# Four scan tiles at the start of an adaLN, attention and FFN kernel: the division by an estimate and one Newton step, and clippings moved to GpSimd

## The reference

```
tf    = sigmoid(sum(time_emb, -1))
decay = exp(-exp(w)) * (0.5 + 0.5*tf)
ek    = exp(min(k, 30));  ekv = ek * v
nf, df = forward scans  a = a*decay + ekv,  b = b*decay + ek
nb, db = the same scans in reverse
euk   = exp(min(u + k, 30))
num   = nf + nb - ekv + euk*v
den   = df + db - ek + euk
out   = sigmoid(r) * num / max(den, 1e-8) * (0.8 + 0.2*tf)
x1    = x + attention(out)          # 16 heads, segments of 128, memory with the delta rule
y     = x1 + ffn(scan2(x1, f, f))   # silu(z W1) * (z W3), Hadamard transform, W2
```

## Time and profile before

| | |
|---|---|
| median of 3 runs | 1583.58 us (1582.86 to 1585.2) |
| profiled execution, span | 1581.4 us |
| PE busy | 1547.0 us, 98% |
| DVE busy | 1219.7 us, 77% |
| ACT busy | 782.1 us, 49% |
| POOL busy | 615.2 us, 39% |

### The profile page before, as it was taken

The page is one execution under the profiler, slowest core; times in us unless marked ns, Lnnn a source line. Parts: engine busy times, 40 slices in busy tenths (PEclk is TensorE's granted clock), DMA queues, the critical chain, the costliest instruction groups (busy, mean ns, idle before and its releaser), DMA issues.

```text
span 1581.4 us, 26868 instructions
## 1 busy us (share of the span) xinstructions
PE 1547.0 (98%) x9574; PEld 1377.9 (87%) x9574; DVE 1219.7 (77%) x2719; ACT 782.1 (49%) x1687; POOL 615.2 (39%) x433
## 2 busy tenths in 40 slices
PE   4899999999999999999999999999999999999999
PEld 2699989999999999998999999989888888888887
DVE  8889888787878888778775773665897888687785
ACT  3576566445535626535546552653554443344442
POOL 3666585322222222222001000134664465666662
PEclk9999999999999999999999999999999999999999
DMA  5375685595473485474467547348211222311111
GB/s 177 124 246 191 223 292 195 180 392 184 161 276 127 154 286 201 147 254 160 174 228 280 210 171 283 110 141 279 88 54 54 60 89 72 107 46 62 54 41 54
DMA packets 109381, 262.04 MB, mean 166 GB/s; under 512 B 11200, under 2 KB 36160, under 8 KB 107840
## 3 DMA queue, kind: packets, MB, share of 16 engines
q1 hardware_dynamic: 90384, 227.28, 40.5%
q10 hardware_dynamic: 18864, 33.04, 6.5%
HBM read 212.03 MB, written 48.25 MB: 165 GB/s over the span
## 4 chain that ended last, share of the span: by engine, by line
PE 90%; DVE 6%; issue 2%; DMA 1%; ACT 1%; POOL 0%; SPq 0%; ACTq 0%; DVEq 0%
PE psG L595 17%; PE psG L597 17%; PE psG L596 17%; PE psX L771 4%; PE psX L726 3%; PE psX L595 3%; PE psX L597 3%; PE psX L596 3%; PE psZ L752 3%; PE psZ L743 3%; PE psZ L751 2%; PE psZ L597 2%; PE psY L597 2%; PE psY L596 2%; PE psZ L596 2%
## 5 line engine op out<-in xcount | busy, mean ns | idle before, releaser
L2076 POOL TENSOR_TENSOR wl<-stage,wh 128x512 fp32r<-128x512 f32 x160 | 233.5, 1481 | 147.4 <-ACT wh L1597 144.7
L595 PE MATMUL psG<-yh,wh 128*128 128x512 f32 x646 | 263.1, 407 | 0.0
L597 PE MATMUL psG<-yh,wl 128*128 128x512 f32 x646 | 253.0, 392 | 0.0
L596 PE MATMUL psG<-yl,wh 128*128 128x512 f32 x646 | 252.1, 390 | 0.0
L2144 POOL TENSOR_TENSOR vs<-v,omb 128x512 f32<-128x512 f32 x64 | 92.1, 1460 | 388.9 <-PE psX L726 216.0
L597 PEld LDWEIGHTS psG<-yh,wl 128*128 128x128 f32 x646 | 121.3, 188 | 26.8
L595 PE MATMUL psG<-wh,yh 128*128 128x256 f32 x480 | 141.6, 295 | 0.0
L595 PEld LDWEIGHTS psG<-yh,wh 128*128 128x128 f32 x646 | 121.9, 189 | 20.9 <-DVE sg L1274 0.3
L596 PEld LDWEIGHTS psG<-yl,wh 128*128 128x128 f32 x646 | 121.9, 189 | 20.5
L597 PE MATMUL psG<-wh,yl 128*128 128x256 f32 x480 | 135.7, 283 | 0.0
L596 PE MATMUL psG<-wl,yh 128*128 128x256 f32 x480 | 135.7, 283 | 0.0
(11 more groups left out here) (279 smaller groups left out, 4291.6 us busy)
## 6 DMA issues: line engine op xcount, KB each, us to landing
wh<-high_o SPq DMA_DIRECT2D x52, 512.0 KB, 3.6
wl<-low_o SPq DMA_DIRECT2D x52, 512.0 KB, 4.7
stage<-in_w SPq DMA_DIRECT2D x64, 256.0 KB, 3.1
wh<-high_k SPq DMA_DIRECT2D x23, 512.0 KB, 3.7
wl<-low_k SPq DMA_DIRECT2D x23, 512.0 KB, 5.0
wh<-high_q SPq DMA_DIRECT2D x23, 512.0 KB, 4.1
wl<-low_q SPq DMA_DIRECT2D x23, 512.0 KB, 5.8
wh<-high_v SPq DMA_DIRECT2D x22, 512.0 KB, 4.0
```

What stands on the lines that cost most here:

```text
L595: e.matmul(out, lh, rh, start=first, stop=False, skip_group_check=check)
L596: e.matmul(out, lh, rl, start=False, stop=False, skip_group_check=check)
L597: return e.matmul(out, ll, rh, start=False, stop=last, skip_group_check=check)
L2076: e.tensor_tensor(lo, raw, hi, ALU.subtract).then_inc(p_wl, 1)
```

## The change

**Division.** For tiles 0 to 3, `oy` no longer follows reciprocals on DVE. ACT computes an estimate r of 1/d as exp(-ln d): `recip(t)` is one activation with Ln and one with Exp, scaled by 2^-37 so that the logarithm stays in range. POOL (`newton(t)`) then multiplies m = num * r and step = d * r, and DVE's `oy` is (2 - step) * m. For tile 0, DVE multiplies m itself (`own_product`). The factor 0.8 + 0.2 tf moves into the gate: `exp_r` gets ln(1/(0.8 + 0.2 tf)) as its bias, and POOL adds 1/(0.8 + 0.2 tf) (`one_more`) where ACT added 1. The first half of tile 3 keeps its two reciprocals on DVE.

**Order on DVE.** `df` of tile 1 stands between `own_product` and `oy` of tile 0, and `df` and `nf` of tile t between `d3` and `oy` of tile t - 1 for t = 2, 3.

**Clippings.** Both clippings of tiles 2 and 3 and the one for exp(u + k) of tile 1 go from DVE to POOL (`clip_k`, `clip_u`, semaphore p_cl). The waits of POOL for `d3` are gone.

**Semaphores.** d_b0 and d_b1 become one, d_z1 and d_zr become one; the sigmoid of the second layer thereby waits for both loads of `z_load`. SP's beta stores wait for v_c 15, which `bo` gives at the end of tile 1.

```diff
             def exp_r(t):
                 if TILES[t][0] == 0:
                     sem, value = er_sem(t)
                     w.wait_ge(sem, value)
-                    e.activation(er_of(t), er_of(t), ACT.Exp, scale=-1.0).then_inc(a_er, 1)
                     if t < 4:
-                        w.wait_ge(a_er, t + 1)
-                        e.activation(er_of(t), er_of(t), ACT.Identity, bias=1.0).then_inc(a_e1, 1)
+                        w.wait_ge(a_c, 4)
+                        e.activation(er_of(t), er_of(t), ACT.Exp, scale=-1.0, bias=ln_over).then_inc(a_er, 1)
...
+            def recip(t):
+
+                _, d, _, r = newton_of(t)
+                w.wait_ge(v_d3, t + 1)
+                e.activation(r, d, ACT.Ln, scale=UNIT).then_inc(a_rc, 1)
+                w.wait_ge(a_rc, 2 * t + 1)
+                e.activation(r, r, ACT.Exp, scale=-1.0, bias=ln_unit).then_inc(a_rc, 1)
...
+            def clip_u(t):
+
+                i, b, c = TILES[t]
+                wait_kx(w, t)
+                w.wait_ge(v_c, 7)
+                w.wait_ge(v_n2, t - 1)
+                w.wait_ge(v_d2, t - 1)
+                e.tensor_scalar(set_of(t)[4], kx_of(t)[:, :], ucut[:, i, c:c + 1], 0.0, ALU.min,
+                                ALU.add).then_inc(p_cl, 1)
+
+            def newton(t):
+
+                m, d, step, r = newton_of(t)
+                w.wait_ge(a_rc, 2 * t + 2)
+                w.wait_ge(v_n2, t + 1)
+                if t > 0:
+                    e.tensor_tensor(m, m, r, ALU.mult).then_inc(p_nr, 1)
+                e.tensor_tensor(step, d, r, ALU.mult).then_inc(p_nr, 1)
...
+                elif name == "oy" and t < 4:
+                    cut = slice(256 if t == 3 else 0, T)
+                    w.wait_ge(p_nr, products(t))
+                    if t == 0:
+                        w.wait_ge(v_rc, 1)
+                    m, _, step, _ = newton_of(t)
+                    e.scalar_tensor_tensor(oys[t][:, cut], step, 2.0, m, ALU.subtract, ALU.mult,
+                                           reverse0=True).then_inc(v_oy, 1)
```

More of the change, by code:

```diff
@@ L1 @@
+import math
 from contextlib import ExitStack
@@ L55 @@
 FIRSTS = [t for t, x in enumerate(TILES) if x[0] == 0]
+LARGE = 1e14
+CLIPPED = {("u", 1): 1, ("k", 2): 2, ("u", 2): 3, ("k", 3): 4, ("u", 3): 5}
+UNIT = 2.0 ** -37
+LN_UNIT = -37 * math.log(2.0)
 SCAN = (("df", 1200), ("nf", 1200), ("er", 0), ("di", 80), ("ni", 80), ("db", 1200), ("mn", 420), ("nb", 1200),
@@ L522, in adaln_attn_ffn, with newton_of, products @@
         ones = S[:, 0, 0:P]
+        over_tf, ln_over, ln_unit = tf[:, 0, :], tf[:, 3, 0:1], tf[:, 3, 1:2]
+        def newton_of(t):
+            cut = slice(256 if t == 3 else 0, T)
+            nf, df, nbk, dbk, _, _ = set_of(t)
+            return nf[:, cut], df[:, cut], nbk[:, cut], dbk[:, cut]
+        def products(t):
+            return 2 * t + 1
         bt, br, bo = (S[:, 1, 16 * i:16 * i + 16] for i in range(3))
@@ L1306, in gains, with own_product @@
                 e.tensor_tensor(first[2], first[0], first[3], ALU.mult).then_inc(v_c, 1)
[L1308 to L1333, removed]
+            def own_product():
+                m, _, _, r = newton_of(0)
+                w.wait_ge(a_rc, 2)
+                w.wait_ge(v_n2, 1)
+                e.tensor_tensor(m, m, r, ALU.mult).then_inc(v_rc, 1)
             def first_half():
@@ L1818, in load_beta @@
                 g = n % NG
-                w.wait_ge(d_b[0], 16)
+                w.wait_ge(d_b, 32)
                 w.wait_ge(v_t2, 6 * n)
@@ L1856, in scalar @@
             exp_u(0)
-            for t in range(4):
-                ends_of(t)
-                if t == 0:
-                    w.wait_ge(d_bt, 16)
-                    e.activation(bt, bt, ACT.Exp, scale=-1.0).then_inc(a_c, 1)
-                exp_k(t + 1 if t < 3 else NT)
-                exp_r(t)
-                if t > 0:
-                    high_y(t - 1)
-                exp_u(t + 1 if t < 3 else NT)
-                if t == 1:
-                    load_ombeta(0)
-                    load_beta(0)
-                if t > 1:
-                    load_k(t + 2)
+            w.wait_ge(v_c, 12)
+            e.activation(ln_over, over_tf[:, 0:1], ACT.Ln).then_inc(a_c, 1)
+            ends_of(0)
+            w.wait_ge(d_bt, 16)
+            e.activation(bt, bt, ACT.Exp, scale=-1.0).then_inc(a_c, 1)
+            exp_k(1)
+            exp_r(0)
+            exp_u(1)
+            recip(0)
+            exp_k(2)
+            exp_r(1)
+            ends_of(1)
+            exp_u(2)
+            high_y(0)
+            exp_k(3)
+            recip(1)
+            exp_u(3)
+            load_ombeta(0)
+            load_beta(0)
+            exp_r(2)
+            ends_of(2)
+            high_y(1)
+            recip(2)
+            load_k(4)
+            exp_r(3)
+            ends_of(3)
+            high_y(2)
+            recip(3)
+            load_k(5)
             load_r(3)
@@ L2167, in gpsimd @@
             ekv(0)
-            w.wait_ge(v_d3, 1)
+            clip_u(1)
             euv(0)
+            one_more(0)
             ekv(1)
+            clip_k(2)
             euv(1)
-            later_rates()
-            for t in range(2, 4):
-                w.wait_ge(v_d3, t)
-                ekv(t)
-                euv(t)
-                low_y(t - 2)
-            w.wait_ge(v_c, 15)
+            newton(0)
+            clip_u(2)
+            one_more(1)
+            ekv(2)
+            low_y(0)
+            clip_k(3)
+            euv(2)
+            later_rates()
+            newton(1)
+            clip_u(3)
+            one_more(2)
+            ekv(3)
+            low_y(1)
+            euv(3)
+            newton(2)
+            one_more(3)
+            low_y(2)
+            newton(3)
+            w.wait_ge(v_c, 16)
             e.tensor_tensor(later[2], later[0], later[3], ALU.mult).then_inc(p_c, 1)
-            w.wait_ge(v_d3, 4)
-            low_y(2)
-            w.wait_ge(v_oh, 1)
             split_w(1)
```

117 lines of the change are left out of this document (79 added, 38 removed).

## The result

The changed kernel takes 1599.34 us (median of four, 1598.47 to 1600.38) against 1583.28 for the kernel before on the same chip: ratio 1.0101, 95% interval 1.0087 to 1.0114. So it is slower by 16.1 us. The prediction said slower by 11.0, 1594.6, with a range that ended at 1598. The sign and the mechanism are the ones it gave; a third of the loss it did not see.

What follows compares the result with a forecast made beforehand. It took DVE to set the first 44 us, through `oy` of tile 2. Turns and the division chain delay that by 3.6 + 4.0 + 3.4 = 11.0 us over tiles 0 to 2: 1583.58 to 1594.6, own range 1591 to 1598, with rival 1 1588 to 1598.

Steps and rivals of the forecast that it cites:

- What bounds the kernel: First 44 us: DVE sets the pace; `oy` of tile 2, at 43.86 us, sets the end, and PE then works without pause.
- First, the turns: Shared DVE and POOL access, first tiles: each waits out the other's data part; 13.4 us of turns a tile against 11.7 now.
- the walk: New instruction lists laid side by side with assumed lengths: `oy` of tiles 0 to 2 at 23.6, 39.8, 54.9; +11.0 us.
- Rival 1: DVE scans in the first tiles give way only in part, the turn taken at their start alone: 1588 to 1590; 5%.
- Second, the chain: From `d3` to `oy`: Ln, table load, Exp, two POOL products and `oy` take 6.0 us; two scans (2.3 us) fill it.
- POOL's one-tensor forms at 0.67 us: POOL's forms with `min` or a pointer, taken at 0.67 us, bounded by 0.61 and 1.26; upper end adds 1.5.
- Rivals 2 and 3: First tiles: 2, no turns but the chain remains, 1585.0, 5%; 3, chain fits behind two scans, 1576, 5% with all between.
- rival 2: First tiles: no turns, the division chain remains, a tile takes 11.9 us, what it takes now: 1585.0, no difference; 5%.
- Rival 4: ACT's table loads: a drain of about 1.38 us after each, five on the path costing 6.9 us more: 1601.5; 3%.

Runs made afterwards that it cites:

- a1: Changed kernel with POOL's nine `min` forms (five clippings, four gate additions) turned into multiply and add, leaving out clippings and cap: 1593.82 us.
- b1: Kernel before with only POOL's waits for `d3` and the one for the first half of tile 3 dropped: 1591.88 us, ratio 1.0055.
- d1: Kernel before with the five clippings on POOL, each in another form, built for its trace to compare their lengths; its one run took 1584.97 us.
- c2: Changed kernel with clippings back on DVE, POOL's gate addition without `min`, and both Newton products moved from POOL to DVE: 1589.32 us.
- a5: Changed kernel with POOL's nine `min` forms as multiply and add, and Identity in place of Ln, so no table loads: 1592.74 us.
- c1: Changed kernel with the clippings back on DVE and POOL's gate addition as multiply and add, without the cap: 1592.44 us.
- b3: Kernel before with six clippings of keys of tiles 1 to 3 moved from DVE to ACT as Relu: 1581.43 us, ratio 0.9989.
- a3: Changed kernel with only POOL's four gate additions turned from `min` and add into multiply and add, pointer kept: 1596.99 us.

## Why the prediction was right in sign and 5 us short

- **What bounds the kernel**: right. The third chunk starts 16.4 us late and the median is 16.1 up: the whole loss lies ahead of that chunk, the main loop is untouched, and tile 3 costs nothing.
- **First, the turns**: right, and in a1, with the assumed forms, right in size too (9.1 us for the six DVE instructions of tile 1, 9.2 in the walk). b1 shows turns alone at 8.8 us. In the changed kernel there are fewer than forecast (8.2 us in place of 9.2), as POOL's slow forms leave it less often at the shared access. Rival 1 (giving way in part) is out: the scan at 35.32 lasts 2.22.
- **Second, the chain**: right in its pieces. Ln is in the trace with 0.63, the load with 1.28, Exp with 0.72. But the prediction's place for the first load, ahead of `d3`, failed in tile 1, since `exp_k` of tile 3 held ACT until 35.61. That cost 0.6 us at most, as POOL was not ready earlier.
- **Failed: a term of the sum**, POOL's one-tensor forms at 0.67 us, bounded by 0.61 and 1.26. They measured 1.99 to 2.88 with their turns, 1.9 to 2.0 without (d1). The step that failed is "I took 0.67, near the first, as it is the same operation with one tensor". The row it leaned on the earlier trace rows is a multiply and an add; the operation in the new instructions is a comparison, and no row of before has one on POOL at this size. A full product was no upper bound for it. a1 gives the price of this term: 5.5 us (1599.3 to 1593.8). d1 gives the reason for the length: the comparison. Why a comparison takes POOL longer is not shown.
- **The walk itself**: with the right forms it was good to 0.6 us at each `oy` (a1), and with the measured lengths put in it the schedule gave all eleven times of the table's experiments to within 2 us. It had the price of the slow forms too low, 4.2 us where a1 has 5.5.
- **Rivals 2 and 3** (no turns; a hidden chain): out by the times (1585.0 and 1576 against 1599.3), by b1, and by the 4.64 us that DVE waits for `oy` of tile 1. c2 comes nearest to rival 2's place, and is still 6.5 us over before.
- **Rival 4** (a drain behind each load): the load at 37.57 ends at 38.85 and the Exp starts at 38.87. So the rule of the Trainium skill ("ScalarE: Activation LUTs", What ACT_TABLE_LOAD costs) of a drain of some 1.38 us doesn't show in any of the loads here.

How the 16.1 us divide depends on the order in which one takes them away. From the changed kernel downwards, each taken against the kernel before of its own group: the length of POOL's comparisons 5.7 (16.1 to 10.4, a1); then the table loads 0.7 (10.4 to 9.7, a5); the 9.7 that are left are turns, order and the rest of the chain. In c1, 9.6 over before without any clipping on POOL, taking the Newton products off POOL gives 3.1 back (c2). The remaining 6.5 of c2 were not divided further; that tile 0 accounts for most of it (4.9 us) is read from the starts, not tried. Nor did a run keep POOL's waits for `d3` beside the new division; b1's 8.8 us are the price of dropping them in the old one, and how much of the 9.6 they make here is open.

## What to carry to other kernels

Before work is moved off the bounding engine, ask what it sheltered: the reciprocals looked like 3.4 us a tile of pure cost, and they were the time in which the neighbour could use the shared access for nothing. Price an instruction by a row of the same operation on the same engine, not by one of the same shape; where there is none, the nearest row of another operation is no upper bound, and if nine instructions depend on it the range has to say so. And where two engines alternate, give the work to the one that holds the access for the shorter time (0.55 us for a three-operand instruction of DVE against 1.10 for a product on POOL), or to a third that takes no part, as ACT in b3. For the first, c2 speaks with 3.1 us, but it doesn't tell the shorter hold from the step between the engines that falls away.

## What the runs showed of the hardware that was not expected

- POOL needed 1.9 to 2.0 us for a 128x512 instruction with a comparison (`min` or `max`) and a second operation, 1.49 us for `min` alone, and 0.62 for multiply and add (d1, one instruction of each form). A pointer in place of an immediate changes nothing visible (a3).
- The forms with `min` and then an addition hold the access that POOL shares with DVE for only part of that time. DVE and POOL of the changed kernel, by start:

```profile
31.42 1.75 DVE L1104 SCALAR_TENSOR_TENSOR qT<-sq,gain,kT 128x512 f32<-128x512 f32 x1
32.71 2.24 POOL L2162 TENSOR_SCALAR EKb<-kxb 128x512 f32<-128x512 f32 x1
33.09 1.09 DVE L1113 SCALAR_TENSOR_TENSOR qT<-qT,etmp 128x512 f32<-128x512 f32 x1
...
46.41 1.99 POOL L2153 TENSOR_SCALAR etmp<-etmp,tf 128x512 f32<-128x512 f32 x1 [1.75 <-ACT etmp L1651]
...
46.51 1.66 DVE L1088 TENSOR_TENSOR_SCAN DBK<-dec,last,DF 128x512 f32<-128x512 f32 x1 [3.64 <-ACT last L1671]
```

`n2` ends at 33.17 and `d3` at 34.18, 1.01 us later. 0.55 of that is the turn of `d3` itself, so the clipping between them held the access for an estimated 0.46 us, as a plain form does (0.47), and yet it runs on to 34.95. The pair below gives the same. The scan is 0.4 us longer than the 1.25 it takes alone and ends at 48.17, ahead of POOL's 48.40; beside a product it would have ended 1.08 after POOL. So DVE was let in at about 48.17 - 1.08 = 47.09 (an estimate), and both ran for over a microsecond. The slow forms thus cost DVE no longer turns; they make POOL's list longer. The Trainium skill ("SBUF — State Buffer", Who interferes with whom) says that the shared pair is an exclusive lock, held for the whole instruction. For products and scans the traces agree (1.08 and 1.10); for these forms they don't. With `min` in second place, one row of d1 speaks for a hold to the end: POOL's instruction ends at 8.19 + 1.94 = 10.13, and DVE's clipping beside it 0.28 later:

```profile
9.57 0.84 DVE L1028 TENSOR_SCALAR EKb<-kx 128x512 f32<-128x512 f32 x1
```

- Each alternation of Ln and Exp brought a table load of 1.28 us. Where it waits for nothing else, the next activation starts 0.01 to 0.02 us behind it.
